# Sums over edges by relation: windows of 16 destinations instead of 64

## The reference, cut to what matters

```
def rgcn_layer(x, src, dst, etype, W, W_root, b, num_rels):
    h = jnp.einsum('ni,rio->rno', x, W)
    msg = h[etype, src]
    seg = dst * num_rels + etype
    sums = jax.ops.segment_sum(msg, seg, num_segments=N * num_rels)
    cnt = jax.ops.segment_sum(jnp.ones(...), seg, num_segments=N * num_rels)
    mean = sums / jnp.maximum(cnt, 1.0)[:, None]
    agg = mean.reshape(N, num_rels, do).sum(axis=1)
    return agg + x @ W_root + b
```

## Time and profile before

| what | us |
|---|---|
| median of 3 runs | 3190.21 (3187.76 to 3191.98) |
| span of the profiled execution | 3796.5 |
| planning, adjacency, dense layers | 985.8 |
| first relation pass | 1291.5 |
| between the passes | 187.2 |
| second relation pass | 1283.0 |
| end | 49.0 |

### The profile page before, as it was taken

The page is one execution under the profiler, slowest core; times in us unless marked ns, Lnnn a source line. Parts: engine busy times, 40 slices in busy tenths (PEclk is TensorE's granted clock), DMA queues, the critical chain, the costliest instruction groups (busy, mean ns, idle before and its releaser), DMA issues.

```text
span 3796.5 us, 67094 instructions
## 1 busy us (share of the span) xinstructions
PE 2410.4 (63%) x19484; PEld 1719.9 (45%) x19484; DVE 2446.7 (64%) x6233; ACT 1055.3 (28%) x2542; POOL 1893.8 (50%) x2063
## 2 busy tenths in 40 slices
PE   4766689988265655555655559945555555555556
PEld 1222244544244544444444447734444444444446
DVE  5989858961466656656666666646565666656667
ACT  2444411112222222222222224422222222222224
POOL 1877710000555555555555541165555555555555
PEclk8888889989576666666566669956666666666668
DMA  1343410241111111111111111111111111111111
GB/s 51 87 105 99 101 41 1 95 122 39 45 40 40 42 41 42 41 41 42 41 42 42 41 33 62 80 44 42 41 41 42 42 41 42 41 42 42 42 42 29
DMA packets 175229, 192.61 MB, mean 51 GB/s; under 512 B 110526, under 2 KB 141137, under 8 KB 174870
## 3 DMA queue, kind: packets, MB, share of 16 engines
q0 software_dynamic: 50048, 102.60, 9.5%
q10 hardware_dynamic: 84924, 40.88, 4.4%
q1 hardware_dynamic: 39898, 44.85, 3.5%
HBM read 130.49 MB, written 38.06 MB: 44 GB/s over the span
## 4 chain that ended last, share of the span: by engine, by line
PE 41%; DVE 26%; another core or an unknown queue 13%; issue 11%; ACT 3%; ACTq 2%; DVEq 1%; DMA 1%; SPq 1%; POOL 1%; POOLq 0%
PE banks L635 27%; DVE adj L1578 13%; DVE hi_hot L1267 4%; PE banks L552 3%; PE banks L567 3%; PE banks L679 2%; ACT adj L1013 2%; DVE lo_hot L1275 2%; PE banks L691 2%; DVE deg_in L1435 2%; DVEq L1576 1%; DMA adj_copy<-adj 1%; DVE adj L1562 1%; SPq L391 1%
## 5 line engine op out<-in xcount | busy, mean ns | idle before, releaser
L635 PE MATMUL banks<-adj 128*128 128x129 f16 x13280 | 1462.9, 290 | 1127.1 <-ACT adj L1013 600.5
L782 POOL DMA_INDIRECT adj<-table,adj x1564 | 1491.4, 954 | 1077.2 <-SPq L441 623.1
L635 PEld LDWEIGHTS banks<-adj 128*128 128x128 f16 x13280 | 1194.6, 131 | 1399.6 <-ACT adj L1013 815.5
L1578 DVE TENSOR_TENSOR adj<-adj,banks 128x516 f32 x1660 | 1147.3, 691 | 1015.9 <-remote 537.7
L1013 ACT ACTIVATE adj<-adj 128x256 f16 x1660 | 636.8, 412 | 1908.6 <-PE banks L635 1050.9
L1562 DVE TENSOR_SCALAR adj<-adj 128x512 f16<-128x512 f16 x1660 | 594.6, 358 | 0.0
L762 POOL TENSOR_SCALAR lo_hot<-minus_iota,zT 128x128 f16<-128x128 f16 x392 | 315.8, 823 | 166.4 <-PE banks L524 105.0
L524 PE MATMUL banks<-hi_hot,lo_hot 128*128 128x400 f16 x977 | 268.4, 382 | 140.5 <-DVE hi_hot L1267 65.8
L1267 DVE TENSOR_SCALAR hi_hot<-iota,zT 128x400 f16<-128x400 f16 x977 | 270.3, 338 | 36.7 <-PE banks L524 36.1
L524 PEld LDWEIGHTS banks<-hi_hot,lo_hot 128*128 128x128 f16 x977 | 101.9, 104 | 307.0 <-issue 253.1
L567 PE MATMUL banks<-adj,split 128*128 128x512 f16 (+1 forms) x1078 | 216.5, 359 | 0.0
(11 more groups left out here) (238 smaller groups left out, 1266.9 us busy)
## 6 DMA issues: line engine op xcount, KB each, us to landing
adj<-table,adj POOLq DMA_INDIRECT x1564
adj_copy<-adj ACTq DMA_DIRECT2D x25, 800.0 KB, 3.8
adj<-adj_copy SPq DMA_DIRECT2D x6, 2176.0 KB, 16.5
table<-adj SPq DMA_DIRECT2D x25, 512.0 KB, 2.6
adj<-adj_copy SPq DMA_DIRECT2D x1, 3072.0 KB, 10.9
adj<-adj_copy SPq DMA_DIRECT2D x3, 1024.0 KB, 15.3
table<-split SPq DMA_DIRECT2D x6, 256.0 KB, 2.3
out_dram<-xres SPq DMA_DIRECT2D x6, 256.0 KB
```

The lines of the kernel that those rows point to most:

```text
L635: m = e.matmul(ps[:, g * CH // 2:g * CH // 2 + b - a], hot[:, j % NHOT, g * P:g * P + P], edge[:, j % NSTG, a:b], start=(q == 0), stop=(q ...
L782: e.indirect_dma_start(gath[:, (t + 1) % NG, :], None, table, bass.IndirectOffsetOnAxis(ap=index[:, which, t:t + 1].bitcast(U32), axis=0)) ...
L1578: e.tensor_tensor(a, a, ps[:, :].rearrange("p (g d) -> p g d", g=G)[:, :, 0:D + 1], ALU.add).then_inc(accumulated, 1)
```

## The change

`WR` becomes 16. A window now has 16 destinations x 8 relations = 128 slots, so one step is one group: the one-hot is 128 x 128, PE makes two matmuls into one bank, and the add is 129 columns wide. There are 196 windows with edges and `JR` = 977 steps. `sums` has 200 windows x 129 columns, the same size as before. The buffers become 8 `edge`, 8 `hot` and 6 banks (`NSUM`).

In a slot tile of 128 the order is now relation x 16 destinations, so eight tiles make a block of 128 nodes, all relations in each. Between the passes the copies to `rowT` read the turned tiles in another order. At the end nothing is folded any more: ACT scales tiles 0, 3 and 6 of a block, POOL tile 2, DVE tiles 1, 4, 5 and 7, each in an operation of its own, and PE adds all eight through `place`, whose eight matrices are now built by folding the identity matrix. PE waits for all three engines before a block.

```diff
-WR, WR_LOG2 = 64, 6
+WR, WR_LOG2 = 16, 4
...
-        NG, NSTG, NHOT = 16, 6, 6
-        NPAIR = 3
-        sums = carve([P, NW4, G, D + 1])
+        NG, NSTG, NHOT = 16, 8, 8
+        NSUM = 6
+        sums = carve([P, NW4, D + 1])
...
-        hot = carve([P, NHOT, G * P // 2], F16)
-        iota_r = carve([P, G * P // 2], F16)
+        hot = carve([P, NHOT, P // 2], F16)
+        iota_r = carve([P, P // 2], F16)
...
-        place = sb("place", [P, REL, P], F32, rel)
+        place = sb("place", [P, WPB, P], F32, rel)
+        fold = sb("fold", [P, P // 2], F32, rel)
...
+        BY_ACT, BY_POOL, BY_DVE = (0, 3, 6), (2,), (1, 4, 5, 7)
...
-                    if j >= NPAIR:
-                        e.wait_ge(accumulated, base + j - NPAIR + 1)
-                    ps = pair[j % NPAIR]
-                    for g in range(G):
-                        for q, (a, b) in enumerate([(D, 2 * D + 1), (0, D)]):
-                            m = e.matmul(ps[:, g * CH // 2:g * CH // 2 + b - a], hot[:, j % NHOT, g * P:g * P + P],
-                                         edge[:, j % NSTG, a:b], start=(q == 0), stop=(q == 1), skip_group_check=True)
+                    if j >= NSUM:
+                        e.wait_ge(accumulated, base + j - NSUM + 1)
+                    for q, (a, b) in enumerate([(D, 2 * D + 1), (0, D)]):
+                        m = e.matmul(bank[j % NSUM][:, 0:b - a], hot[:, j % NHOT, :], edge[:, j % NSTG, a:b],
+                                     start=(q == 0), stop=(q == 1), skip_group_check=True)
...
-                for w in range(nb * WPB, (nb + 1) * WPB):
-                    _, _, slots, act_at, dve_at = slots_of(w)
-                    e.wait_ge(scaled_act, act_at)
-                    e.wait_ge(slots_added, dve_at)
-                    for g in slots:
-                        m = e.matmul(to, place[:, w % WPB * G, :], sums[:, w, g, 0:D], start=False,
-                                     stop=(w % WPB == WPB - 1 and g == 3), skip_group_check=True)
+                e.wait_ge(scaled_act, (nb + 1) * len(BY_ACT))
+                e.wait_ge(scaled_dve, (nb + 1) * len(BY_DVE))
+                e.wait_ge(scaled_pool, (nb + 1) * len(BY_POOL))
+                for k in range(WPB):
+                    m = e.matmul(to, place[:, k, :], sums[:, nb * WPB + k, 0:D], start=False, stop=(k == WPB - 1),
+                                 skip_group_check=True)
...
-            for a in range(0, P, WR):
-                for w in range(WPB):
-                    e.tensor_copy(place[a:a + WR, w * G:(w + 1) * G, w * WR:(w + 1) * WR],
-                                  ident[a:a + WR, a:a + WR].unsqueeze(1).broadcast_to([WR, G, WR])).then_inc(place_set, 1)
-                    e.wait_ge(place_set, a // WR * WPB + w + 1)
+            half = ident[:, :]
+            for i, n in enumerate((P // 2, P // 4, WR)):
+                if i:
+                    e.wait_ge(own_pool, 1 + i)
+                e.tensor_tensor(fold[:, 0:n], half[:, 0:n], half[:, n:2 * n], ALU.add).then_inc(own_pool, 1)
+                half = fold[:, 0:n]
+            e.wait_ge(own_pool, 4)
+            for k in range(WPB):
+                e.tensor_copy(place[:, k, k * WR:(k + 1) * WR], fold[:, 0:WR]).then_inc(place_set, 1)
...
-            for w in range(NW4):
-                e.tensor_scalar(sums[:, w, 2, 0:D], sums[:, w, 2, 0:D], inv[:, w * G + 2:w * G + 3], None,
-                                ALU.mult).then_inc(scaled_pool, 1)
+            for nb in range(NB):
+                for k in BY_POOL:
+                    w = nb * WPB + k
+                    e.tensor_scalar(sums[:, w, 0:D], sums[:, w, 0:D], inv[:, w:w + 1], None, ALU.mult).then_inc(scaled_pool, 1)
...
-                    v = bank[h][:, :].rearrange("p (r n) -> p r n", n=WR)
-                    hi = rowT[:, s, 0, 0:REL, h * WR:(h + 1) * WR]
+                    v = bank[h][:, :].rearrange("p (k r n) -> p r k n", r=REL, n=WR)
+                    hi = rowT[:, s, 0, 0:REL, h * P // 2:(h + 1) * P // 2].rearrange("p r (k n) -> p r k n", n=WR)
...
-                    a = sums[:, bass.ds(c, 1), :, :].rearrange("p o g d -> p (o g) d")
-                    e.tensor_tensor(a, a, ps[:, :].rearrange("p (g d) -> p g d", g=G)[:, :, 0:D + 1],
-                                    ALU.add).then_inc(accumulated, 1)
+                    a = sums[:, bass.ds(c, 1), :].rearrange("p o d -> p (o d)")
+                    e.tensor_tensor(a, a, bank[j % NSUM][:, 0:D + 1], ALU.add).then_inc(accumulated, 1)
...
-                    e.scalar_tensor_tensor(out=sums[:, w, g, 0:D], in0=sums[:, w, g, 0:D],
-                                           scalar=inv[:, w * G + g:w * G + g + 1], in1=sums[:, w, g - 1, 0:D],
-                                           op0=ALU.mult, op1=ALU.add).then_inc(slots_added, 1)
+            def scale_slots(nb):
+                for k in BY_DVE:
+                    w = nb * WPB + k
+                    e.tensor_scalar(sums[:, w, 0:D], sums[:, w, 0:D], inv[:, w:w + 1], None, ALU.mult).then_inc(scaled_dve, 1)
```

More of the change, by code:

```diff
@@ L85, in gnn_stack @@
         bank = [banks[:, i, :] for i in range(8)]
-        pair = [banks[:, 2 * i:2 * i + 2, :].rearrange("p a b -> p (a b)") for i in range(4)]
+        turned = [banks[:, 2 * i:2 * i + 2, :].rearrange("p a b -> p (a b)") for i in (2, 3)]
         ident = sb("ident", [P, P], F32)
@@ L235, in gnn_stack @@
         adj_ctx.close()
-        sums_g = sums[:, :, :, :].rearrange("p w g d -> p (w g) d")
         sq1, sqr = zT[:, 0:RR * H], zT[:, RR * H:RR * H + HB * D]
@@ L334, in gnn_stack @@
         FRONT = 4
+        BY_ACT, BY_POOL, BY_DVE = (0, 3, 6), (2,), (1, 4, 5, 7)
+        assert sorted(BY_ACT + BY_POOL + BY_DVE) == list(range(WPB))
         def final_by_act(b):
             return b < 4 * FRONT or (b - 4 * FRONT) % (7 - FRONT) == 0
-        def slots_of(w):
-            mine = ((0,), (1, 3), (1, 3)) if w % 2 == 0 else ((0, 1), (3,), (0, 1, 3))
-            return mine + (w + 1 + (w + 1) // 2, 2 * (w + 1) - (w + 1) // 2)
         def final_place(b):
@@ L657, in turn_rows @@
             def turn_rows(nb):
-                g0 = nb * GB
+                g0 = nb * WPB
                 for h in range(2):
@@ L1087, in _ @@
             e.wait_ge(inv_set, 2)
-            for w in range(NW4):
-                for g in slots_of(w)[0]:
-                    e.activation(sums[:, w, g, 0:D], sums[:, w, g, 0:D], ACT.Identity,
-                                 scale=inv[:, w * G + g:w * G + g + 1]).then_inc(scaled_act, 1)
+            for nb in range(NB):
+                for k in BY_ACT:
+                    w = nb * WPB + k
+                    e.activation(sums[:, w, 0:D], sums[:, w, 0:D], ACT.Identity, scale=inv[:, w:w + 1]).then_inc(scaled_act, 1)
             def final_rows(b0, b1):
@@ L1583, in relation_sums @@
                         between(j - REGS)
-                cnt = sums[:, :, :, D].rearrange("p w g -> p (w g)")
+                cnt = sums[:, :, D]
                 e.wait_ge(accumulated, base + JR)
@@ L1696, in turn_rows @@
                 for h in range(2):
-                    v = bank[h][:, :].rearrange("p (r n) -> p r n", n=WR)
-                    hi, lo = (rowT[:, s, q, 0:REL, h * WR:(h + 1) * WR] for q in range(2))
+                    v = bank[h][:, :].rearrange("p (k r n) -> p r k n", r=REL, n=WR)
+                    hi, lo = (rowT[:, s, q, 0:REL, h * P // 2:(h + 1) * P // 2].rearrange("p r (k n) -> p r k n", n=WR)
+                              for q in range(2))
                     e.wait_ge(row_high, 2 * nb + h + 1)
@@ L1755, in final_stats @@
                 own.up()
-            for w in range(2 * WPB):
-                add_slots(w)
+            for nb in range(2):
+                scale_slots(nb)
             for nb in range(NB):
-                for w in range((nb + 2) * WPB, min((nb + 3) * WPB, NW4)):
-                    add_slots(w)
+                if nb + 2 < NB:
+                    scale_slots(nb + 2)
                 final_stats(nb)
```

38 lines of the change are left out of this document (14 added, 24 removed).

## The result

The changed kernel takes 3203.28 us (median of 4 runs, 3203.07 to 3204.44), the kernel before beside it 3190.31 (3187.76 to 3191.98). The ratio is 1.0043, 95% interval 1.0029 to 1.0058: 13 us slower.

A forecast was written before the change was run, and what follows sets the result against it. POOL's gathers, 1.25 us each, were taken to pace both passes before and after. Terms +16.7 end, +2.6 plan, -2.2 and -2 passes, +1 middle sum to +16.1: 3206 us, range 3182 to 3221.

The forecast's parts named there:

- plan (start of the first gather): Before the passes: step list grows from 318 to 465 columns, lengthening DVE operations and PE's picks; +2.6 us, bounds +1.5 to +4.
- middle stage: Between the passes: new order of copies out of PSUM on ACT and DVE, which have room; 0 to +3, taken as +1 us.
- end stage: After the passes: PE places eight tiles a block instead of five, 0.67 us more on each of 25 blocks; +16.7 us.
- two passes: Shorter matmuls and add behind each pass's last gather, -2.2 us in all; less delay by consumers, another -2 us.
- POOL's pace: In both passes gathers come one by one, 1.25 us each; a pass lasts 980.8 us, already before the change.
- the lower bound: End stage: +15 us if scaling and PE start sooner than now.
- The rival of a slow clock: PE stays at the low clock level through the end, 100 us of matmuls instead of 54, some 3250 us; chance 0.03.
- The path of the consumers: In the passes after the change, without POOL's cover: 0.55 us a step over 977 steps.
- The 218 us a pass: DVE's path in a pass shrinks from 830 x 0.91 to 977 x 0.55 us, worth nothing beside POOL.
- I take these pauses for an effect of the profiler: Consumers' repeated pauses in the passes, 89 times 3.0 us in the first, were left out of a pass's cost.
- the unexplained 606.3 us: Profiled execution 3796.5 us against median 3190.2, almost the 623.1 us that POOL waited for slots.
- The rival that the pauses are partly real: Passes carry 38 us over POOL's pace, which the lighter consumers give back: 3170 us; faster by more excess, chance 0.12.

The follow-up runs named there:

- half_before: The kernel before with every second gather left out from the 17th tile on, on a 3796 us chip: 2948.6 us.
- half_after: The changed kernel with every second gather left out from the 17th tile on, on a 3796 us chip: 2595.3 us.
- after_again: The changed kernel itself, run once more unedited on a 3796 us chip: 3641.27 us, ratio 0.9593 to the kernel before.

## Why the prediction was right, and where it was wrong

**The forecast held:** 3203.3 us against 3206, inside 3182 to 3221, slower as 0.75 of the chances had it. Here is the sum by term; what was measured is the profile after less the stages of the earlier trace rows, and for the passes what is left:

| term | predicted | measured |
|---|---|---|
| plan (start of the first gather) | +2.6 | +0.8 |
| middle stage | +1 | +2.5 |
| end stage | +16.7 | +15.2 |
| two passes | -2.2 and -2 | -4.3 |
| sum | +16.1 | +14.2 |

The passes of before on a 3190 chip are inferred: 3190.2 less 1.8 us between span and time (3204.4 less 3202.6) less 1222.0 leaves 983.2 each, and those of after are 981.2 and 980.9, where the sum had 980.8. The 1.2 us between 14.2 and the measured 13.0 are the profiled run against the median. No trace of the kernel before on a 3190 chip exists, so that its passes go at POOL's pace there is argued: they come out within 4 us of the changed kernel's, which do, and 781 periods of 1.249 us are 975.5 us, below which no pass can go. The split between plan and passes is soft as well. The first gather starts at 985.8, 980.2 and 981.9 us in the three traces with the old plan and at 984.0 to 987.8 in the eleven with the new one, so the plan can be worth 4 us as well as 0.8, and the passes then -7.5 instead of -4.3. It is partly luck that the total is so near: the end was 1.5 us less than forecast and the middle 1.5 us more.

**The mis-sized terms.** The end: blocks are 2.01 us apart as forecast, but the other operations around the 25 blocks gave 1.5 us back, as the lower bound had allowed. DVE's four scalings take 1.03 us, 0.26 each, where the sum took the 0.363 of the folding operation, so DVE, priced at 1.93 us a block, was never near PE's 2.01. The rival of a slow clock fell too: 0.90 was granted in the end stage. Its price was mis-added: 225 matmuls at 0.223 us are 50, not 54. The plan: the operations grew as priced, and the first matmul of the adjacency stage starts 3.1 us later, within the forecast's bounds. That the first gather starts only 0.8 us later may be no more than the spread of the traces. Timelines of PE, the kernel before and the changed one:

```profile
94.31 4.24 PE L524 MATMUL banks<-hi_hot,lo_hot 128*128 128x400 f16 x14 [11.80 <-SPq L394]
```

```profile
97.38 2.85 PE L517 MATMUL banks<-hi_hot,lo_hot 128*128 128x400 f16 x8 [12.96 <-SPq L387]
```

The middle: the price was looked for in the order of the copies, where it isn't; it came from where `rowT` lies. The path of the consumers, put at 0.55 us a step, is 0.595. The 218 us a pass that the change was said to take from it are 757 less 582 = 175 by that; the 757 of the kernel before was not measured alone. half_before less half_after is 353 us, which is twice 175 and 1, but both totals hold pauses, so it is no check.

**The step that failed** is "I take these pauses for an effect of the profiler". The sum needed only that they are not there in the runs behind 3190.2 us, which fits all that was measured, and the unexplained 606.3 us were taken for the same execution with and without a profiler. They were two kinds of chips. "Remote" in the earlier trace rows was no sign of a cause either: in that trace only some 1150 increments by the 1660 adds are recorded, and a wait whose releaser has no record has to be put down to something else. So the forecast that the profiled span falls by up to 600 us and the median doesn't follow came true in its number (3796.5 to 3202.6) for a wrong reason: the span of a run is 1.8 to 2.0 us under its time on either kind. The rival that the pauses are partly real was priced as if one time had to hold both, 3170 us. In fact it goes by the chip: on a 3190 chip there is no sign of them, on a 3796 chip they are in every run, and there the change makes the kernel 4.1% faster. Two numbers for one kernel that differ by 19% are a question to settle first, not a term to explain away.

**What each engine then decides.** On a 3190 chip a pass has a gather every 1.25 us, so work taken there from DVE and PE is worth nothing, and the f32 matmuls added to the end, where PE is the bound, cost in full. On a 3796 chip the consumers' path with its slow hand-overs is the bound, and the change, which makes it shorter, gains 173 us in the passes and pays 19 elsewhere.

**Open:** what delays PE's increments. Shown is that the pauses come with the gathers, that data is not late, and that the recording alone doesn't make them. SP's relay, the landing increments, the descriptors, and the recording together with something of these chips were not told apart on a chip that has the pauses. The traces hold one hint: on the 3796 chips most increments in the passes have no record. Each of the 16 gather semaphores has some 1568 recorded increments in the profile after (two have 1537), 154 to 277 in after_again. It isn't only the gathers: of the 1954 adds, each of which increments once, all are recorded in the one and some 860 in the other. Outside the passes the records are complete on both. So the recording suffers on these chips where the pauses are, as cause, as effect or beside them. It also means that "who waited for whom" is less sure in those traces than start times are. Why two chips do it and two don't wasn't to be seen.

## What to carry to other kernels

Before costing a change, find the engine that sets the pace and its period, and ask whether the profile and the median were taken under one condition: here the same edit is worth -153 or +13 us by which engine is the bound. Match an instruction with the one that it waits for by counting, not by nearness in the timeline, as an engine can be several steps ahead. Work removed beside a fixed instruction price (1.25 us a gather, of which half the rows save 0.05) brings nothing; what brings something is fewer such instructions. Trading a fold on idle engines for matmuls is paid in full where PE sets the stage, 0.22 us for each 128 x 128 f32 matmul.

## What the hardware showed that was not expected

- One kernel, two times, by chip: 3186 to 3193 us in all runs on two chips and on that of the result, 3788 to 3804 in all runs on two others. The excess stands only in the passes, and half_before and half_after lose most of it with half of the gathers.
- A gather of 128 rows takes 0.945 us, one of 64 rows 0.899: it is nearly all fixed.
- The same 1350 matmuls take 81.0 us when the operand in `rowT` starts at a multiple of 64 bytes from the start of its memory (80.3 to 81.3 us in four traces) and 83.2 to 84.5 us in the ten traces where it doesn't.
- On a 3796 chip PE's increment came 5.0 us (median of 538 adds) after the start of the matmuls that it tells of, on a 3190 chip 0.41 us.
- Four times the matmuls in the passes raised the granted clock there from 0.50 to 0.72 of full speed.
